# Recurrent block with a gated two-layer local-attention network on one core: the first tiles' exponentials and key copies in another order, and the last gated input later

## The reference, cut to what matters

```python
xn = layernorm(x)                                # 16 sequences x 512 rows x 128, fp32
s  = recurrence(xn)                              # conv of width 4, two gates, scan over the rows, W_out, rms norm
f  = xn
for l in range(2):                               # two layers
    h = shift_token(f)                           # half of the features moved by one row
    q, k, v = split(h @ wqkv[l], 3)              # 8 heads of 64
    q, k = rotate(l2norm(q) * qs[l]), rotate(l2norm(k) * ks[l])
    f = f + local_attention(q, k, v) @ wo[l]     # windows of 64 rows, each sees itself and the one before
    h = layernorm(shift_token(f)) * lg[l] + lb[l]
    a, g = split(h @ w1[l] + b1[l], 2)
    f = f + (a * gelu(g)) @ w2[l] + b2[l]
out = x + s * silu(f)

# in the recurrence
xc  = causal_conv(xn)
r_t = sigmoid(xc @ W_r.T + b_r); i_t = sigmoid(xc @ W_i.T + b_i)
inp = i_t * xc                                   # the gated input, one 128 x 512 tile for each sequence
```

## Time and profile before

| what | value |
|---|---|
| median of three runs | 1308.66 us (1307.43, 1308.66, 1312.0) |
| the profiled execution's own time | 1307.07 us |
| its span, first to last instruction | 1305.3 us |
| busy share of the span: PE, PEld | 96%, 77% |
| DVE, ACT, POOL | 84%, 89%, 88% |
| instructions | 38178 |
| mean granted TensorE clock | 0.999 |

### The profile page before, as it was taken

One profiled execution on the slowest core, in us unless ns is written; L12 is line 12 of the kernel. 1 busy time (PEld: TensorE's weight loads), 2 busy tenths in 40 slices (PEclk: granted clock), 3 DMA queues, 4 the chain that ended last, 5 costly groups with the idle time before them and its releaser, 6 DMA issues.

```text
span 1305.3 us, 38178 instructions
## 1 busy us (share of the span) xinstructions
PE 1258.8 (96%) x13794; PEld 1006.3 (77%) x13794; DVE 1090.7 (84%) x1883; ACT 1162.4 (89%) x3529; POOL 1145.7 (88%) x840
## 2 busy tenths in 40 slices
PE   7999999999999999899978999999999999999998
PEld 4778888888888887566656788888888888876776
DVE  6888888888888886699878898989889998883777
ACT  5889999999999998887768899999999999998886
POOL 4999999999999987499779999999999999984776
PEclk9999999999999999999999999999999999999999
DMA  5222222222222211011011122122122221110223
GB/s 168 54 63 63 62 62 63 63 66 73 63 71 71 56 41 35 17 35 36 1 30 36 41 53 47 46 47 46 46 48 54 54 46 46 38 39 25 70 76 97
DMA packets 60298, 70.04 MB, mean 54 GB/s; under 512 B 8912, under 2 KB 38288, under 8 KB 60112
## 3 DMA queue, kind: packets, MB, share of 16 engines
q1 hardware_dynamic: 60112, 67.61, 20.8%
HBM read 13.33 MB, written 4.19 MB: 13 GB/s over the span
## 4 chain that ended last, share of the span: by engine, by line
PE 75%; POOL 10%; DVE 5%; ACT 4%; issue 4%; DMA 1%; SPq 0%; DVEq 0%; ACTq 0%; POOLq 0%
PE ps L203 59%; PE ps L268 8%; POOL t L1263 4%; PE ps L278 3%; PE ps L281 3%; POOL hxr L1263 2%; ACT P L657 2%; POOL P L1263 1%; DVE t L979 1%; POOL side L1293 1%; DVE t L991 1%; DVE nm L1010 1%; DMA B<-in_wqkv 0%; ACT sqk L631 0%; PE ps L445 0%
## 5 line engine op out<-in xcount | busy, mean ns | idle before, releaser
L657 ACT ACTIVATE P<-ps,nm 128x128 f32<-128x128 f32 x1024 | 364.4, 385 | 2.3 <-DVE nm L1010 1.9
L203 PE MATMUL ps<-wqkv,hT 128*128 128x512 f32 x1152 | 329.2, 427 | 15.5 <-DVE t L979 11.8
L1263 POOL TENSOR_TENSOR t<-t 128x1024 f32<-128x1024 f32 x128 | 307.5, 2403 | 34.4 <-DVE t L979 31.7
L1263 POOL TENSOR_TENSOR P<-P,rden 128x512 f32<-128x512 f32 x256 | 292.4, 1152 | 23.5 <-DVE rden L1017 21.6
L203 PEld LDWEIGHTS ps<-wqkv,hT 128*128 128x128 f32 x1152 | 214.5, 188 | 94.9 <-issue 28.2
L1263 POOL TENSOR_TENSOR t<-t,rr 128x1024 f32<-128x1024 f32 x128 | 244.2, 1908 | 18.6 <-ACT rr L640 18.4
L657 ACT ACTIVATION_READ_ACCUMULATOR P<-ps,nm 128x1 f32 x1024 | 230.6, 225 | 0.0
L991 DVE TENSOR_TENSOR t<-ps,tabl 128x512 f32<-128x512 f32 x256 | 164.2, 682 | 41.2 <-ACT sqk L631 39.7
L1263 POOL TENSOR_TENSOR hxr<-hxf,hxr 128x512 fp32r<-128x512 f32 (+1 forms) x93 | 131.0, 1437 | 67.0 <-ACT hxr L713 67.0
L1010 DVE TENSOR_REDUCE nm<-ps 128x4 f32<-128x512 f32 x256 | 173.4, 679 | 5.2 <-PE ps L203 5.1
L647 ACT ACTIVATE PT<-ps 128x1024 f32<-128x1024 f32 x128 | 130.6, 1020 | 51.1 <-PE ps L268 50.0
(11 more groups left out here) (140 smaller groups left out, 2544.1 us busy)
## 6 DMA issues: line engine op xcount, KB each, us to landing
Vs<-Vn SPq DMA_DIRECT2D x224, 128.0 KB, 2.4
side<-in_x SPq DMA_DIRECT2D x17, 256.0 KB, 3.0
A<-X SPq DMA_DIRECT2D x16, 256.0 KB, 2.5
norm<-X SPq DMA_DIRECT2D x32, 128.0 KB, 2.2
norm<-X SPq DMA_DIRECT2D x32, 127.8 KB, 2.4
hsh<-X SPq DMA_DIRECT2D x31, 128.0 KB, 2.3
hsh<-X SPq DMA_DIRECT2D x31, 127.8 KB, 2.3
oT<-in_x SPq DMA_DIRECT2D x15, 256.0 KB, 3.0
```

The lines of the kernel that those rows point to most:

```text
L203: return e.matmul(o, lhsT, rhs, start=start, stop=stop, skip_group_check=True)
L657: k = act(P[:, g, :], ps[:, 3 + s, (g % 4) * 128:(g % 4 + 1) * 128], ACT.Exp, bias=nm[:, g:g + 1], accum_out=den[:, g:g + 1])
L1263: return e.tensor_tensor(o, a, b_, op)
```

## The change

On ACT, both layers: the first half of the exponentials of tile 0 moves within step 2 from the end of the step to a place ahead of `square` of tile 2. On DVE, both layers: the key copy of tile 1 moves from step 3 into step 2, behind `rotate` of tile 2 and ahead of its `norm_sum`. On DVE, layer 1 only: the key copy of tile 0 moves from step 1 to a place between the second and the third part of `rotate` of tile 1; both `row_max` of tile 0 go ahead of `norm_sum` of tile 1; and `gates2(15)` moves from the end of layer 0 to layer 1's step 2, behind `norm_sum` of tile 2. For its sake `keep_o` of tile 0 in layer 1 gets a wait.

```diff
@@ keep_o (scalar)
                 if b:
                     e.wait_ge(s_wo, 2 * (m - 1) + t // 2 + 1)
+                elif l and t == 0:
+                    e.wait_ge(s_xi, NB)
@@ scalar, step i
+                    if i == 2:
+                        exps(l, 0, 0)
                     if l < i < NT:
                         square(l, i)
@@ scalar, end of step i
-                    if 0 <= i - 2 < NT:
+                    if 0 < i - 2 < NT:
                         exps(l, i - 2, 0)
@@ vector, step i
-                    if 0 < i - 2 < NT:
+                    if 1 < i - 2 < NT:
                         keep_k(l, i - 2)
@@ vector, step i, behind rotate
-                    if i == 1:
+                    if i == 1 and l:
+                        row_max(l, 0, 0)
+                        row_max(l, 0, 1)
+                    elif i == 1:
                         keep_k(l, 0)
+                    if i == 2:
+                        keep_k(l, 1)
                     if i < NT and (i or not l):
                         norm_sum(l, i)
-                    if i == 1:
+                    if i == 1 and not l:
                         row_max(l, 0, 0)
                         row_max(l, 0, 1)
+                    if l and i == 2:
+                        gates2(NB - 1)
@@ vector, last round of layer 0
                             down_add(0, NB - 1)
-                            for p in range(3):
+                            for p in range(2):
                                 rotate(1, 1, p)
+                            keep_k(1, 0)
+                            rotate(1, 1, 2)
@@ vector, the rounds of layer 0
-                    if l == 0 and b < NB:
+                    if l == 0 and b < NB - 1:
                         gates2(b)
```

## The result

| | before | changed |
|---|---|---|
| median of 22 runs each | 1310.74 us | 1313.87 us |
| ratio, 95% interval | | 1.0028 (1.0017 to 1.0039), 2.2 to 5.1 us |
| measured again, 12 runs | | 1.0020 (1.0008 to 1.0032) |
| profiled execution, own time, span | 1307.07, 1305.3 us | 1315.01, 1313.2 us |
| mean granted TensorE clock | 0.999 | 0.995 |

The changed kernel is slower, by about 3 us. The forecast had 2.2 us and called it nothing that can be told.

The account below looks back on a forecast made before the run. Bound: PE in the long stretches, with the two ramps ahead passing delays on through POOL's `add_qk` of tile 2. +0.2 (layer 0), +1.94 (layer 1) and 0.1 (gated input) gave +2.2 us on 1308.66: 1310.9 us, range 1306.8 to 1314.2.

Parts of the forecast that it names:

- The order in layer 1: Layer 1's ramp: the later sum of tile 1 and the earlier exponentials delay the squares of tile 2, +1.94 us.
- The order in layer 0: Layer 0's ramp: the earlier exponentials make the squares of tile 2 0.58 us later, `add_qk` of tile 2 +0.2 us.
- 0.38 of the 0.58 is hidden by the transfer and the work behind it: Layer 0's ramp: of the squares' 0.58 us delay, only 0.2 us reaches POOL's `add_qk` of tile 2.
- The gated input: Layer 1: `gates2(15)` ahead of tile 0's first inverse costs 0.1 us, bounds 0 and about +0.5.
- From 680 on every step of the old chain still follows that addition, in the old order, so I see no place that gives it back: Layer 1 after `add_qk` of tile 2 on POOL: the delay stays unchanged to the end of the span.
- The sum: Whole kernel: +0.2, +1.94 and 0.1 make +2.2 us, 1310.9 us against the median 1308.66.
- No difference that can be told: Whole kernel: 2.2 us is 0.17%, under the 0.3% (3.9 us) a measurement can tell; chance of within 0.80.
- the chance of 0.16 for "slower": Whole kernel: chance 0.16 of being slower by over 0.3%, that is over 1312.6 us.
- Rival 3, the clock: Layer 1, 673 to 680: PE's clock falls after two idle gaps, +2.5 us on top of 2.2; 1314 us, chance 0.08.
- Rivals 1 and 2: Delay swallowed in ramp 690 to 731, 1308.9, chance 0.15; layer 1's earlier products reach the end, 1307.2, chance 0.12.

Follow-up runs that it names:

- a_again: The changed kernel again, unaltered; ratio 1.0020 to the kernel before.
- e_layer1: The changed kernel with layer 0's exponentials and key copy put back as before, so layer 1's part alone; ratio 1.0028 to the kernel before.
- e_gated_late: The changed kernel with `gates2(15)` in layer 1's step 4, ahead of the key copy of tile 2; ratio 1.0021 to the kernel before.
- e_layer0: The kernel before with only the change's layer 0 part (early exponentials of tile 0, key copy of tile 1 in step 2); ratio 1.0020.
- e_layer0_fill: The kernel before with the change's layer 0 part, plus 16 and 5 small matmuls in PE's two idle gaps of layer 0's ramp; ratio 1.0000.
- b_third: The kernel before, unaltered, measured a third time; ratio 1.0003.
- e_layer0_2: The kernel before with the change's layer 0 part alone, measured a second time; ratio 1.0008.
- e_exps_alone: The kernel before with only the exponentials of tile 0 moved ahead of the squares of tile 2, in both layers; ratio 1.0021.

## Why the prediction was right and wrong

- **The order in layer 1**: +1.94 forecast, +1.96 measured, and each half of it within 0.02 us in five kernels. The products of queries and keys of tile 0 came 1.43 us earlier, as worked out; 1.01 of it reaches the rotation of tile 2 once both orders are undone. Right.
- **The order in layer 0**: +0.2 forecast. 0.1 to 0.2 measured against the first profile, but 0.5 against executions in which the transfer was not late, five of seven. The "0.38 of the 0.58 is hidden by the transfer and the work behind it" was read from one trace that has it and was taken as a property of the kernel. Mis-sized in most executions.
- **The gated input**: this step failed, as a term of the sum that was sized too small. The prediction took 0.1, with 0.5 as its upper bound "if it also lengthens POOL's two instructions beside it". It lengthened one of them: 0.46. I had asked when the inverse is usable and whether POOL waits for it, and it is usable in time. The cost came by another way, POOL's own next instruction getting slower. The trace before had such a pair: `rec_root` ended at 687.28, 0.55 us after POOL's scaling, and POOL's addition behind it took 2.82 us where others take 2.38. The Trainium skill (GPSIMD Engine Reference, table of section 1) says that both engines share interfaces to SBUF and that DVE instructions with two SBUF inputs contend; by it the forecast had the sum 0.1 to 0.5 us larger. The trace agrees: 0.46 measured, 0.36 more than was taken.
- **"From 680 on every step of the old chain still follows that addition, in the old order, so I see no place that gives it back"**: nothing was given back, but 0.3 us more were lost. The shift alone did not do it (with the clock up `rec_root` takes 1.58 us and nobody waits); the clock's fall did, by way of the rotation of tile 3 and `rec_root`.
- **The sum**: 2.2 forecast. In layer 1's ramp 1.96 + 0.46 + 0.3 = 2.72 us, in layer 0's 0.1 to 0.5, so 2.8 to 3.2 together, and clock falls in layer 0's ramp that come and go with either kernel; timed 3.7 and 2.6 us. The forecast's time of 1310.9 is 3.0 us under the median of 22 runs; 2.1 of these are its base, a median of three runs that lay that much under the one of 22.
- **"No difference that can be told"**: wrong, and the second step that failed. 2.2 us of 1308.66 is 0.17%, and I took 0.3% as the limit. With 22 runs each the interval (1.0017 to 1.0039) excludes 1.0, and with the terms above the loss sits next to that limit. Its sign had been worked out; the chance of 0.16 for "slower" left it too far down.
- **Rival 3, the clock**: its event took place in the stretch where it was put, in all three traces with this layer 1 (changed, `a_again`, `e_layer1`), and in `e_gated_late`. Not by the way it was put: I wanted two gaps of 2.2 and 2.1 us with little between them, since 2.8 us of idleness at the kernel's end had left the clock up. It fell behind the first, of 2.19, and 0.59 us more, before the second, which was then only 1.24. Its price was wrong as well: 2.5 us on the path forecast, 0.3 measured. I had priced PE's doubled work without asking who waited for it. The rule of the Trainium skill (TensorE: Matmul & The Clock Gate, The HAM clock gate) that idleness brings the throttle back agrees with these rows (granted clock 0.99 from 680 to 682, 0.50 from 682 to 684).
- **Rivals 1 and 2** fell: the delay is still there 500 us later (the last rotation of layer 1 stands 500.09 us behind its first before, 502.71 changed; 499.46 and 500.50 in the repeats of the one, 503.56 in that of the other).

## What to carry to other kernels

When an instruction is moved on an engine that works in order, look first at what waits for the one it now stands ahead of: here the exponentials were moved ahead of squares that the whole ramp hung on, while their own user had not moved. Price a move also by what runs beside the new place: DVE and POOL instructions on SBUF lengthened each other by 0.5 to 2.1 us here. Count a clock fall by who waits for PE at that place: it cost 0.3 us at one place and 2.2 us a few microseconds later. And a wait that hides a delay in one trace has to be seen in a second one before it is counted on: the late transfer of layer 0 was there in two executions of seven.

## What the runs showed of the hardware that was not expected

- The clock's fall is not a property of the program alone. The ramp of layer 1 that the kernel before has ran at full clock in four executions (two of the kernel before, `e_layer0`, `e_layer0_fill`) and fell in two (`b_third`, `e_layer0_2`, +0.3 us each).
- The length of a gap alone does not decide. `e_exps_alone` had a gap of 2.11 us in its layer 1 ramp, with PE busy for only 0.20 us of two, and kept 1.00, while others fell behind gaps of 2.12 us. Windows of `e_exps_alone`:

```profile
679.86:681.86 2.00, 0.20 (x1) 0.21 (x2) 2.00 (x4) 1.66 (x9) 0.18 (x1) 1.00 0.78 184
```

- One DVE instruction on two SBUF inputs, of the same shape and on the same data (`gates2(15)`, `A<-oT`), took 0.68, 1.14 and 2.77 us, by what POOL did beside it. What decides is when POOL's running instruction ends: in the layer 1 ramps of all eighteen traces there are 64 cases of `gates2` or `rec_root` starting beside one, and every one of them ends 0.54 to 0.56 us after it. A POOL instruction that starts meanwhile ends late in turn (`rec_a2` 1.50 for 1.04, an addition 2.82 for 2.38). That reads as taking turns rather than as both running slower; no run here tests it by itself.
